# All products of u first in TensorE's slot, and ScalarE's first half of the exponentials ahead of the carry copy

## The reference, cut to what matters

```python
dt = softplus(proj[..., :512] + dt_bias)          # per position and inner channel
Bm, Cm = proj[..., 512:576], proj[..., 576:]      # 64 states
A = -exp(A_log)
def step(hst, ins):                                # over 256 positions
    dt_t, B_t, C_t, x_t = ins
    dA = exp(dt_t[:, :, None] * A)                 # the exponentials
    hst = hst * dA + (dt_t * x_t)[:, :, None] * B_t[:, None, :]   # "u" is the second summand
    y_t = einsum('bds,bs->bd', hst, C_t)
    return hst, y_t
```

## Time and profile before

| what | value |
|---|---|
| median of 3 runs | 5366.41 us (5361.21 to 5369.36) |
| the profiled execution | 5370.79 us, of which the trace spans 5369.1 us |
| TensorE busy | 4970.5 us (93%), 44784 matmuls |
| VectorE busy | 4726.2 us (88%), of it the 2048 scans 4540.7 us |
| ScalarE busy | 3415.8 us (64%) |
| GpSimd busy | 3751.7 us (70%) |
| mean granted TensorE clock | 0.987 of full |
| scans | first starts at 108.2 us, last at 4910.3 us |

### The profile page before, as it was taken

How to read it: one execution, slowest core, us unless ns; L and a number is a source line. 1 busy time by engine, 2 the same in 40 slices (tenths; PEclk the granted TensorE clock), 3 DMA queues, 4 the chain that set the end, 5 groups by cost and what they waited for, 6 DMA issues and landing times. The chain is left out here.

```text
span 5369.1 us, 130492 instructions
## 1 busy us (share of the span) xinstructions
PE 4970.5 (93%) x44784; PEld 2522.5 (47%) x44784; DVE 4726.2 (88%) x2419; ACT 3415.8 (64%) x11498; POOL 3751.7 (70%) x6613
## 2 busy tenths in 40 slices
PE   6999999999999999999999999999999999886898
PEld 4444444444444444444444444444444444443444
DVE  2999999999999999999999999999999999996443
ACT  4666766666666766666676766666676766663112
POOL 4777768677777868777776868677776868674211
PEclk8999999999999999999999999999999999998899
DMA  3121111111121111112121111111121211113441
GB/s 106 38 64 43 54 48 52 54 39 61 38 64 42 55 48 52 55 38 61 38 64 43 61 41 52 55 37 61 39 63 39 64 38 43 36 29 104 146 153 66
DMA packets 433144, 306.75 MB, mean 57 GB/s; under 512 B 215920, under 2 KB 336240, under 8 KB 432496
## 3 DMA queue, kind: packets, MB, share of 16 engines
q1 hardware_dynamic: 428272, 294.39, 18.2%
q10 hardware_dynamic: 4224, 4.19, 0.2%
HBM read 187.27 MB, written 111.15 MB: 56 GB/s over the span
## 5 line engine op out<-in xcount | busy, mean ns | idle before, releaser
L891 DVE TENSOR_TENSOR_SCAN b_hs<-b_dA,b_u 128x1024 f32<-128x1024 f32 x2048 | 4540.7, 2270 | 273.9 <-ACT b_u L818 187.0
L1056 PE MATMUL b_ex<-b_dd,b_aw 32*128 32x512 f32 x8192 | 2710.1, 642 | 33.7 <-POOL b_dd L534 15.4
L1043 PE MATMUL b_u<-b_ud,b_bw 32*128 32x256 f32 x16384 | 2336.5, 401 | 258.9 <-DVE b_hs L891 237.6
L800 ACT ACTIVATE b_dA<-b_ex 128x496 f32<-128x496 f32 x4096 | 2289.7, 589 | 145.4 <-PE b_ex L1056 142.6
L1043 PEld LDWEIGHTS b_u<-b_ud,b_bw 32*128 32x128 f32 x16384 | 1425.9, 184 | 1119.1 <-issue 635.5
L1075 PE MATMUL b_y<-b_hs,b_cw 128*32 128x256 f32 x16384 | 1309.9, 390 | 2.3 <-DVE b_hs L891 2.3
L818 ACT ACTIVATE b_u<-b_hin 128x32 f32<-128x32 f32 x1792 | 364.7, 203 | 1192.2 <-PE b_u L1043 1006.9
L534 POOL TENSOR_TENSOR b_dd<-b_dr,b_mask 128x512 f32<-128x512 f32 x1024 | 1073.2, 1048 | 52.2 <-DVE b_hs L891 39.4
L543 POOL TENSOR_TENSOR b_ud<-b_ur,b_mask 128x512 f32<-128x512 f32 x1024 | 1083.5, 1058 | 0.0
L1056 PEld LDWEIGHTS b_ex<-b_dd,b_aw 32*128 32x128 f32 x8192 | 856.6, 183 | 106.7 <-ACT b_dA L800 65.9
L570 POOL TENSOR_TENSOR b_hm<-b_first,b_hs 128x32 f32<-128x32 f32 x1792 | 480.1, 268 | 539.4 <-ACT b_first L799 517.8
(11 more groups left out here) (104 smaller groups left out, 2283.1 us busy)
## 6 DMA issues: line engine op xcount, KB each, us to landing
b_u<-scratch_ut SPq DMA_DIRECT2D x256, 128.0 KB, 2.9
scratch_y<-b_ysb SPq DMA_DIRECT2D x128, 256.0 KB, 2.3
scratch_xs<-b_xs SPq DMA_DIRECT2D x64, 256.0 KB, 2.4
scratch_sz<-b_sd SPq DMA_DIRECT2D x64, 256.0 KB, 2.2
scratch_dt<-b_sd SPq DMA_DIRECT2D x64, 256.0 KB, 2.1
scratch_ut<-b_uT SPq DMA_DIRECT2D x64, 256.0 KB, 2.4
b_ur<-scratch_ut SPq DMA_DIRECT2D x1024, 16.0 KB
b_dr<-scratch_dt SPq DMA_DIRECT2D x1024, 16.0 KB, 1.7
```

The costliest lines, as they stand in the source:

```text
L800: nc.scalar.activation(dA[:, j % NDA, h, :, 1:TC], src[:, :, 1:TC], ACT.Exp).then_inc(exp_done, 1)
L891: nc.vector.tensor_tensor_scan(hs[:, v, :, :, kp].rearrange("p d t -> p (d t)"), dA[:, j % NDA, :, :, :].rearrange("p h d t -> p (h d t)") ...
L1043: ins = nc.tensor.matmul(dst[:, :, tb, :], bw[row(r), c % 2, tb, :], ud[row(r), j // 2 % NPR, tb, :, :], start=(tb == 0), stop=(tb == NTB ...
L1056: nc.tensor.matmul(e[bank_of[what]][:, :], aw[row(r), p % DIRS, v, :, :].rearrange("p b s -> p (b s)"), dd[row(r), (p * PAIRS + j // 2) % ...
```

## The change

Three functions are edited. On ScalarE, `decay(p, j)` becomes `decay(p, j, h)` and does one half per call; the waits for scan j - 4 and for the carried state are in the call for half 0. In `one_pass` the exponentials of half 0 of step j + 2 are put ahead of the carry copy of step j, and those of half 1 stay behind it. On TensorE, `step` issues all four products of u and then the two exponents, where before it issued two products of u, one exponent, two products of u, one exponent. No instruction is added or left out; the start-up calls keep their order.

```diff
-                def decay(p, j):
+                def decay(p, j, h):
                     c, k, kp, v = place(j)
-                    act.wait_ge(scanned, scanned_to(p, j - NDA))
+                    if h == 0:
+                        act.wait_ge(scanned, scanned_to(p, j - NDA))
+                        if c:
+                            act.wait_ge(hin_made, hin_to(p, j - NM))
+                    src = e[bank_of["e", 2 * (p * JP + j) + h]][:, :].rearrange("p (d t) -> p d t", t=TC)
+                    act.wait_ge(e_done[2 * (1 - kp) + h], p * (JP // 2) + (j // 2 + 1))
                     if c:
-                        act.wait_ge(hin_made, hin_to(p, j - NM))
-                    for h in range(2):
-                        src = e[bank_of["e", 2 * (p * JP + j) + h]][:, :].rearrange("p (d t) -> p d t", t=TC)
-                        act.wait_ge(e_done[2 * (1 - kp) + h], p * (JP // 2) + (j // 2 + 1))
-                        if c:
-                            nc.scalar.activation(e0[:, j % NM, h, :], src[:, :, 0], ACT.Exp).then_inc(e0_done, 1)
-                        nc.scalar.activation(dA[:, j % NDA, h, :, 1:TC], src[:, :, 1:TC], ACT.Exp).then_inc(exp_done, 1)
+                        nc.scalar.activation(e0[:, j % NM, h, :], src[:, :, 0], ACT.Exp).then_inc(e0_done, 1)
+                    nc.scalar.activation(dA[:, j % NDA, h, :, 1:TC], src[:, :, 1:TC], ACT.Exp).then_inc(exp_done, 1)
...
                         half = (p * JP + j) // HALF
+                        then = (p, j + 2) if j + 2 < JP else None if last else (p + 1, j + 2 - JP)
+                        if then:
+                            decay(*then, 0)
                         if j >= STEPS:
                             put_carry(p, j)
-                        if j + 2 < JP:
-                            decay(p, j + 2)
-                        elif not last:
-                            decay(p + 1, j + 2 - JP)
+                        if then:
+                            decay(*then, 1)
...
                     for tb in range(NTB):
                         for h in range(2):
                             inject(p, j, h, tb)
-                        if then:
-                            exponent(*then, tb)
+                    if then:
+                        for h in range(2):
+                            exponent(*then, h)
```

More of the change, by code:

```diff
@@ L831, in one_pass @@
                         next(side, None)
-                decay(0, 0)
-                decay(0, 1)
+                for j in range(2):
+                    for h in range(2):
+                        decay(0, j, h)
                 for p in range(PASSES):
```

## The result

| kernel | median us (lowest to highest) | ratio to the kernel before, 95% interval |
|---|---|---|
| before | 5366.46 (5361.21 to 5369.36) | |
| changed | 5536.38 (5533.45 to 5537.74) | 1.0317 [1.0299, 1.0335] |

The change makes the kernel 170 us slower. The profiled execution took 5535.85 us, its span is 5534.1 us, 165.0 us more than before.

What follows compares the result with a forecast made beforehand. VectorE's scans, with gaps ended by the carry copy, set the pace. 0.44 us at 380 places makes 167 us; with at most some 10 us for later exponents, +170 us takes 5366.4 to 5536 us, range 5450 to 5665.

Steps and rivals of the forecast that it cites:

- The bound and the loop: VectorE's scans set the pace; the loop through TensorE's u and the carry copy goes from 3.98-4.11 to 4.51-4.64 us.
- The 0.53 us: On ScalarE, the half 0 exponentials ahead of the carry copy make it 0.53 us later in TensorE's step.
- the banks are unmoved: Half 1's exponentials start as late as before, so bank use stays, except half 0's bank comes free 0.14 us earlier.
- No gain for u: On TensorE, the new product order brings u no gain: its products still end 1.13 us into the step.
- rival 1: TensorE's exponents start only behind the last product of u; 502 us lost, 5870 us or more, chance 0.07.
- rivals 2 and 3: Exponents end 0.2 us before u, copy keeps its slack, 5366 us, chance 0.04; or 0.53 us before, 5273 us, chance 0.05.
- rival 3: TensorE's exponent ends at least 0.53 us before u, ScalarE's half 0 fits its wait; 5273 us, chance 0.05.
- The sum: On VectorE, 0.44 us lost at each of 380 gaps ending with the carry copy: 167 us, forecast +170 us.
- The eight scans: A worked stretch of VectorE scans, said to lose 1.32 us over three gaps that end with a copy.
- What I looked for: Signs: copy at +1.87 us, VectorE's idle behind it some 350 us at more places, ScalarE's wait moved, busy times unchanged.
- some 350: VectorE's idle time behind the carry copy would go from 187 us to some 350 us, at far more than 380 places.
- Busy times unchanged: A sign that the forecast is right: the engines' busy times stay as before.

Runs made afterwards that it cites:

- e1: Changed kernel with TensorE's old order of products put back, so ScalarE's half of the change alone: 5486.52 us, 1.0219 of the kernel before.
- e2: Kernel before with TensorE's half of the change alone, all products of u first and ScalarE's order as before: 5330.64 us, 0.9933.
- e5: Changed kernel with exponent 0 issued before TensorE waits for scan j-2: 5405.81 us, 1.0061 of the kernel before.
- e4: Changed kernel with only half 0's first-position exponential ahead of the copy: 5389.21 us; sorting: quiet if TensorE starts within 2.6 us of the awaited scan's start, otherwise late.
- e9: Changed kernel with TensorE's exponent of half 0 issued between the last two products of u: 5501.46 us, 1.0251 of the kernel before.

## Why the prediction was right, point by point

- **The bound and the loop.** Right. The copy was what VectorE waited for, the exponentials had time, and the copy moved from 1.34 to 1.87 us of TensorE's step, as worked out.
- **The 0.53 us.** Right as a total, wrong in its parts. What stands ahead of the copy takes 0.54 us (2393.72 to 2394.26), and the first exponential starts 0.01 us before the moment at which the copy used to. I had this from an exponent ending with u at 1.14, plus 0.21 us of latency. In fact with the old TensorE order the exponential can start at 1.26 us (e1), and the new order delays its report by 0.077 us and its start to 1.33 us. The two errors, some 0.08 us each, cancel in the changed kernel only, and that is luck. Taken apart, ScalarE's half is +0.46 us and 117.5 us, and TensorE's half on top of it 50 us, of which I had booked 10. That "the banks are unmoved" was wrong too: TensorE's waits for them went from 71.1 to 14.9 us, without a gain in the time.
- **"No gain for u".** Wrong: u is reported 0.05 us earlier, and e2 is 38 us faster. That this gain is lost in the changed kernel, since the copy no longer follows u, was right.
- **Products in program order (rival 1).** Its condition isn't met: the starts pass each other, as in the earlier trace rows. The rule of the Trainium skill, "TensorE: Matmul & The Clock Gate", Part 3, The mechanism, says that starts and ends keep program order. Of its two halves this trace refutes the one on starts (2392.41 ahead of 2392.71) and bears out the one on ends, as far as the reports show. I had thrown out both.
- **Hidden, and faster (rivals 2 and 3).** No exponent was done 0.2 or 0.53 us before u, and neither happened. e5 shows a part of what rival 3 asked for: with exponent 0 done earlier on quiet steps the loss falls from 170 to 37 us. It doesn't turn into a gain: they are not earlier where TensorE is late, and TensorE waits for banks more.
- **The sum.** The total of 167 us hit, but the term behind it doesn't hold, so that it hit is luck. The eight scans lost 0.82 us and not the 1.32 us that I worked out. The first six scans lost what I said to within 0.05 us (0.53, 0, 0, 0, then 0.23 and 0.31 where I had 0.27 and 0.26). The seventh gave back 0.78 us instead of 0.46: its wait for TensorE's sums went away in full. The last then lost 0.54 us for my 0.73. At 0.27 us for each of three gaps, 380 gaps would make 104 us. What fills the sum up are places that are new, 297 of them by the list of waits, to a large part in quiet stretches, which I named in the loop (0.06 to 0.13 us a scan) but didn't add. By the sorting used for e4, the start distances beyond 2.19 us went from 90 to 179 us in the quiet steps and from 217 to 285 us in the late ones: about half of the loss in each, and so with any limit from 2.5 to 2.8 us. Better would have been the loss per scan: 0.82 / 8 x 1792 = 184 us, beside 170 measured.
- **What I looked for.** The copy's place, ScalarE's wait and the small new gaps came as said; the gap time of 319.3 us at 677 places is near the "some 350". "Busy times unchanged" missed: VectorE's scans stand 52.5 us longer in the profile, 41 us of it from lost overlap, and this is a third of the loss.

## What to carry to other kernels

Moving work into an engine's wait pays only if that work is ready before the awaited thing. Look up when the moved instruction's own input is done, and at which steps. Here it was made in the same step as what the engine waited for. Where this loop has 0.3 to 0.4 us to spare on quiet steps, a delay of 0.15 us still cost 59 us, at least half of it at steps where TensorE came late. Judge an order by its late steps as well as its quiet ones, and count what each wait in an engine's instruction stream (here for a bank) holds behind it.

## What the runs showed of the hardware that was not expected

TensorE reports products of different row groups in program order, even though they start out of that order: six matmuls of u were passed by the exponents at the start of a step. By the semaphore events, the four reports of a step (two halves of u, two exponents) came in the order of issue in each of the 1947 steps counted in each of the eleven traces, whichever of four orders the kernel used, and mostly 0.043 us apart. The modelled ends in the profile don't show it (1.15 and 1.16 us for exponents whose reports differ by 0.077 us). Where ScalarE waits for the exponent first, the exponential follows its report by 0.104 us: medians of 1.148 and 1.253 us in e1, 1.182 and 1.287 in e9, 1.225 and 1.329 in the changed kernel. So for a product on which something waits, its place among products that run beside it is worth some 0.04 us for each one ahead: exponent 0 is reported at 1.148, 1.182 and 1.225 us with none, one and both halves of u ahead of it.
